# A two-layer graph convolution on one core: halved last chunk of each layer, and a prologue whose x reads, slot lists and order test stand elsewhere

## The reference

```python
norm = _cheb_norm(src, dst, x.shape[0])
h = jnp.maximum(_layernorm(x, axis=-1), 0.0)
# _cheb_conv(x, W0, W1, b): prop gathers h[src], scales by norm, sums by dst
out = x @ W0
tx1 = prop(x)
out = out + tx1 @ W1
return out + b
...
h = _cheb_conv(x, src, dst, norm, W1_0, W1_1, b1)
h = _layer_norm(h, gamma, beta)
h = jnp.where(h >= 0, h, NEG_SLOPE * h)
out = _cheb_conv(h, src, dst, norm, W2_0, W2_1, b2)
# the kernel returns x + out
```

## Time and profile before

| | us |
|---|---|
| median of three runs | 2506.06 |
| lowest, highest | 2500.96, 2516.93 |
| the profiled execution | 2524.07 |
| its span, first to last instruction | 2522.2 |

### The profile page before, as it was taken

The page is one execution under the profiler, slowest core; times in us unless marked ns, Lnnn a source line. Parts: engine busy times, 40 slices in busy tenths (PEclk is TensorE's granted clock), DMA queues, the critical chain, the costliest instruction groups (busy, mean ns, idle before and its releaser), DMA issues.

```text
span 2522.2 us, 25703 instructions
## 1 busy us (share of the span) xinstructions
PE 2030.6 (81%) x6734; PEld 1107.1 (44%) x6734; DVE 1412.3 (56%) x3392; ACT 1486.9 (59%) x2720; POOL 1491.0 (59%) x1574
## 2 busy tenths in 40 slices
PE   3358878888888788788877888787888888878787
PEld 3334434444444444444434444444444444444444
DVE  9736656666666666666654445354445454545444
ACT  8537656666666666666654555455555455555554
POOL 0166666666666666666636656666666666656662
PEclk9979999999999999899998889999999899989999
DMA  9977676766677677667747666666676667666662
GB/s 224 267 252 205 201 207 195 205 200 201 204 205 204 202 204 205 191 199 208 203 126 225 197 204 209 216 209 212 211 214 209 208 209 218 208 195 213 214 215 93
DMA packets 195754, 516.14 MB, mean 205 GB/s; under 512 B 44343, under 2 KB 46030, under 8 KB 195612
## 3 DMA queue, kind: packets, MB, share of 16 engines
q0 software_dynamic: 125120, 411.69, 55.7%
q1 hardware_dynamic: 67664, 102.43, 13.1%
q10 hardware_dynamic: 2828, 0.44, 0.1%
HBM read 473.61 MB, written 40.84 MB: 204 GB/s over the span
## 4 chain that ended last, share of the span: by engine, by line
ACT 28%; PE 24%; another core or an unknown queue 23%; issue 14%; DVE 7%; DMA 1%; SPq 1%; ACTq 0%; POOL 0%; DVEq 0%; POOLq 0%
PE ps L1161 12%; ACT high L629 7%; ACT ps L629 6%; ACT ps L630 5%; PE ps L1312 4%; ACT high L630 4%; PE ps L1305 3%; PE ps L1303 3%; DVE low L981 2%; ACT work L670 2%; DVE low L985 1%; ACT hots_full L581 1%; PE ps L1156 1%; PE ps L1248 1%
## 5 line engine op out<-in xcount | busy, mean ns | idle before, releaser
L525 POOL DMA_INDIRECT arena<-table,idx_all x1550 | 1473.7, 951 | 899.3 <-issue 486.1
L985 DVE TENSOR_TENSOR low<-arena,ps 128x512 fp32r<-128x512 f32 x517 | 339.0, 680 | 523.0 <-ACT ps L630 254.5
L1303 PE MATMUL ps<-high,hots 128*128 128x512 f32 x1034 | 583.1, 564 | 0.2 <-issue 0.2
L981 DVE SCALAR_TENSOR_TENSOR low<-arena,ps 128x512 fp32r<-128x512 f32 x517 | 372.5, 742 | 307.6 <-ACT ps L629 185.2
L1312 PE MATMUL ps<-arena,hots_full 128*128 128x512 f32 x1060 | 527.5, 596 | 0.0
L1305 PE MATMUL ps<-low,hots 128*128 128x512 f32 x1034 | 423.0, 409 | 50.5 <-DVE low L981 26.4
L629 ACT ACTIVATE high<-arena 128x512 fp32r<-128x512 f32 x517 | 368.0, 712 | 15.2 <-remote 15.2
L629 ACT ACTIVATE ps<-arena 128x512 fp32r<-128x512 f32 x517 | 354.2, 685 | 31.6 <-DMA arena<-table,idx_all 29.3
L630 ACT CAST ps<-arena 128x512 fp32r<-128x512 f32 x517 | 305.5, 591 | 87.6 <-DVE low L985 66.5
L1161 PE MATMUL ps<-arena 128*128 128x512 f32 x424 | 235.8, 708 | 133.5 <-ACT arena L662 128.1
L630 ACT CAST high<-arena 128x512 fp32r<-128x512 f32 x517 | 320.5, 620 | 0.0
(11 more groups left out here) (153 smaller groups left out, 1531.3 us busy)
## 6 DMA issues: line engine op xcount, KB each, us to landing
arena<-table SPq DMA_DIRECT2D x106, 256.0 KB
arena<-table,idx_all POOLq DMA_INDIRECT x1550
table<-arena SPq DMA_DIRECT2D x53, 256.0 KB
arena<-in_x_dram SPq DMA_DIRECT2D x53, 256.0 KB
out_dram<-arena SPq DMA_DIRECT2D x53, 256.0 KB
table<-arena SPq DMA_DIRECT2D x10, 1120.0 KB
arena<-in_x_dram SPq DMA_DIRECT2D x9, 1120.0 KB
w_all<-in_L_gnn_W_dram SPq DMA_DIRECT2D x2, 1024.0 KB
```

The costliest lines, as they stand in the source:

```text
L525: nc.gpsimd.indirect_dma_start(out=rows[u][:, c, 0:RW if L == 0 else D], out_offset=None, in_=table[L][0:NEAR if near else N, :], in_offse ...
L981: nc.vector.scalar_tensor_tensor(out=low[a], in0=rows[u][:, c, 0:D], scalar=rows[u][:, c, D:D + 1], in1=high_ps[s % NB][:, :], op0=ALU.mul ...
L985: nc.vector.tensor_tensor(low[a], rows[u][:, c, 0:D], high_ps[s % NB][:, :], ALU.subtract).then_inc(s_low, 1)
L1303: nc.tensor.matmul(tx_ps[u][:, :], hot, high[a], start=c == 0, stop=False)
```

## The change

The line numbers of the changed kernel differ. In the prologue, x groups 1 to 10 are read through GpSimd's queue; SyncE reads group 0 alone and has the slot lists between the table stores; `idx_all`, the order test and the bases stand ahead of the node scales on VectorE, and the transpose of `dst_rows` stands last on TensorE; GpSimd's wait for the table stands inside the branch.

```diff
@@ sync
-            for g in range(NG):
-                for n0, n1 in parts:
-                    sp.dma_start(nodes[n0:n1, XG[g]:XG[g + 1], :], x_rows[n0:n1, XG[g]:XG[g + 1], :],
-                                 max_dma_last_dim=4 * D).then_inc(s_x[g], 16)
+            for n0, n1 in parts:
+                sp.dma_start(nodes[n0:n1, XG[0]:XG[1], :], x_rows[n0:n1, XG[0]:XG[1], :],
+                             max_dma_last_dim=4 * D).then_inc(s_x[0], 16)
...
-            slot_rows(src, idx_all, s_idx)
-            slot_rows(dst, dst_rows, s_dsts)
             for g in range(1, NG):
+                if g == 3:
+                    slot_rows(src, idx_all, s_idx)
+                elif g == 5:
+                    slot_rows(dst, dst_rows, s_dsts)
@@ gpsimd
+            for g in range(1, NG):
+                for n0, n1 in ((0, TA), (TA, TR)):
+                    pool.dma_start(nodes[n0:n1, XG[g]:XG[g + 1], :], x_rows[n0:n1, XG[g]:XG[g + 1], :],
+                                   max_dma_last_dim=4 * D).then_inc(s_x[g], 16)
...
             bad = pool.value_load(flag_i[0:1, 0:1], min_val=0, max_val=1)
-            pool.wait_ge(s_tab, 2 * 16 * (NG - 1))
-            pool.wait_ge(s_factor_out, 48)
@@ gpsimd, layer(L) and general(L), L == 0
+                    pool.wait_ge(s_tab, 2 * 16 * (NG - 1))
+                    pool.wait_ge(s_factor_out, 48)
@@ vector
             nc.vector.reciprocal(factors[:, :, 0], sqrt_veps_deg).then_inc(s_factor, 1)
+            dve.wait_ge(s_idxps, 1)
+            nc.vector.tensor_copy(idx_all[:, 0:4 * P], src_ps[0][:, :]).then_inc(s_idxr, 1)
...
+            order()
+            bases()
```

```diff
+        def products(i, u):
+            if i < NC - 1:
+                return [(mm_ps[u][:, :], bass.ds(0, D))]
+            return [(mm_ps[u][:, 0:HD], bass.ds(0, HD)), (tx_ps[1 - u][:, 0:HD], bass.ds(HD, HD))]
@@ tensor
                     slots(i, u, h, 6, 11)
...
+                    if i == NC - 1:
+                        carried(L, u)
                     slots(i, u, h, 11, SLOTS)
...
-                    else:
-                        carried(L, u)
@@ scalar
                 chunks_of(act_step)
+                take_tx(L, NC - 1, 0)
+                copy_txT(L, NC - 1)
                 if L == 0:
                     make_sloped(NC - 2, 1)
-                take_tx(L, NC - 1, 0)
-                copy_txT(L, NC - 1)
@@ vector, finish2
-                nc.vector.scalar_tensor_tensor(out=mm_ps[u][:, :], in0=mm_ps[u][:, :], scalar=scale(i, 5),
-                                               in1=xin[u], op0=ALU.mult, op1=ALU.add).then_inc(s_res, 1)
...
-                nc.vector.tensor_tensor(stage, mm_ps[u][:, :], bias2, ALU.add).then_inc(s_fin, 1)
+            def residual2(i, u, h):
+                dve.wait_ge(s_xr[u], 16 * (h + 1))
+                nc.vector.tensor_tensor(xin[u], xin[u], bias2, ALU.add).then_inc(s_res, 1)
...
+                    last = nc.vector.scalar_tensor_tensor(out=stage[:, cols], in0=mm, scalar=scale(i, 5),
+                                                          in1=xin[u][:, cols], op0=ALU.mult, op1=ALU.add)
```

More of the change, by code:

```diff
@@ L524, in layer @@
                         n = first_slot(i) + c
+                        rn = REST if n == S - 1 else P
                         nc.gpsimd.indirect_dma_start(
-                            out=rows[u][:, c, 0:RW if L == 0 else D], out_offset=None, in_=table[L][0:NEAR if near else N, :],
+                            out=rows[u][0:rn, c, 0:RW if L == 0 else D], out_offset=None, in_=table[L][0:NEAR if near else N, :],
                             in_offset=bass.IndirectOffsetOnAxis(
-                                ap=(idx_near if near else idx_all)[:, n:n + 1].bitcast(U32), axis=0),
+                                ap=(idx_near if near else idx_all)[0:rn, n:n + 1].bitcast(U32), axis=0),
                         ).then_inc(s_gath[u][c], 16)
@@ L832, in tile_mean @@
                 dve.sem_inc(s_dpass, 1)
-                norm.add(nc.vector.bn_aggr(mv[0:TR, :], stats[0:TR, :]))
+                norm.add(nc.vector.bn_aggr(mv[0:TR, :], stats[0:TR, 0, :]))
             def tile_relu(t):
@@ L887, in _ @@
                                   dst_rows[0:S - FB * P, FB * P:]).then_inc(s_dstrows, 1)
-            order()
-            bases()
             dve.wait_ge(s_locps, 1)
@@ L1062, in norm1 @@
                 epi.settle(dve)
-                nc.vector.scalar_tensor_tensor(out=mm_ps[u][:, :], in0=mm_ps[u][:, :], scalar=veps[:, 1:2],
-                                               in1=bet, op0=ALU.mult, op1=ALU.add).then_inc(s_h1, 1)
-                assert epi.n == K_EPI
+                for mm, cols in products(i, u):
+                    nc.vector.scalar_tensor_tensor(out=mm, in0=mm, scalar=veps[:, 1:2], in1=bet[:, cols], op0=ALU.mult,
+                                                   op1=ALU.add).then_inc(s_h1, 1)
@@ L1067, in finish1 @@
+                assert epi.n == K_EPI + (3 if i == NC - 1 else 0)
             def finish1(i, u):
[L1069 to L1075 removed]
+                for n, (mm, cols) in enumerate(products(i, u)):
+                    dve.wait_ge(s_slope, i + 1 + n)
+                    if n == 0:
+                        dve.wait_ge(s_tab1, 16 * (i + 1))
+                    dve.sem_inc(s_dpass, 1)
+                    last = nc.vector.scalar_tensor_tensor(out=stage[:, cols], in0=mm, scalar=scale(i, 2),
+                                                          in1=sloped[:, cols], op0=ALU.mult, op1=ALU.max)
@@ L1088, in layer @@
+                last.then_inc(s_fin, 1)
             def layer(L):
@@ L1304, in slots @@
                             pe.wait_ge(s_low, split_no(L, i, c) + 1)
-                            last = nc.tensor.matmul(tx_ps[u][:, :], hot, low[a], start=False, stop=i == NC - 2 and c == SLOTS - 1)
+                            last = nc.tensor.matmul(tx_ps[u][:, :], hot, low[a], start=False, stop=i >= NC - 2 and c == SLOTS - 1)
                         else:
```

104 lines of the change are left out of this document (66 added, 38 removed).

## The result

| | before | after |
|---|---|---|
| median of 20 runs, us | 2515.24 | 2505.02 |
| lowest, highest | 2499.65, 2523.11 | 2482.57, 2518.61 |
| ratio, 95% interval | | 0.9963 (0.9947 to 0.9980) |
| span of the profiled execution | 2522.2 | 2480.7 |

The changed kernel is 0.37% faster, 9.3 us, and three further comparisons gave 0.9948 (0.9921 to 0.9976), 0.9969 (0.9947 to 0.9991) and 0.9960 (0.9936 to 0.9984): 0.40% on the mean of the four, 10 us. The forecast was −9.7 us, 0.39%. The spans differ by 41.5 us, but the trace of after is of the fastest of its 20 executions and that of before, 2524.07, is above all 20 of before, so they must be read place by place.

What follows compares the result with a forecast made beforehand. GpSimd's successive gathers were taken to fill the middle, with SyncE's late issues holding up the prologue. Terms of −6, −1.8 and −1.9 sum to −9.7 us, from a median of 2506.06 to 2496.4 us, range 2484 to 2510.

Steps and rivals of the forecast that it cites:

- no change: Whole kernel: a result within about 1%, 25 us, of before, given 0.84; faster by that 0.10, slower 0.06.
- The sum: Whole kernel: prologue −6, layer 0's end −1.8 and layer 1's end −1.9 make −9.7 us.
- Prologue, −6: Before the first gather: SyncE, freed of x reads, issues the factors at about 97, not 103.32; bounds −1 and −8.
- First slot: After the first gather: VectorE's later last step may hold the first slot back a microsecond, covered by gathers running on.
- The start is passed on: From prologue to total time: the prologue's −6 us enters the sum in full.
- Layer 0's end, −1.8: Layer 0's tail: earlier carry products −0.9, last operation in two halves −0.9; bounds −0.5 and −8.
- Layer 1's end, −1.9: Layer 1's tail: carry −0.9, one 256-column operation behind dense_tx −1.0; bounds −1 and −3.
- the DMA engines limit the prologue: Prologue: transfers, not SyncE's issues, set the end; only 1 to 3 us come through, about 2500; chance 0.25.
- GpSimd starved by VectorE: Prologue: x reads wait for one-hots, 9.2 us a group and no gain, or about 2540 at double price; chance 0.06.
- The residual add: Layer 1's chunks: the early add delays gather issues by up to 0.69 us each, about 2504, 2533 in full; chance 0.10.
- The fourth rival: Layer 0's end: the copy's remote wait and slow dense_tx both go, −3.2 and −3.1, about 2490; chance 0.20.

Runs made afterwards that it cites:

- pause_each: The changed kernel with one tiny GpSimd operation, waited for, after every gather; 1.0064 (1.0037 to 1.0090) of the kernel before.
- reads_only: The kernel before with only x groups 1 to 10 read through GpSimd's queue, SyncE reading group 0; 0.9975 (0.9958 to 0.9992) of before.
- prologue_only: The kernel before with only the change's edits ahead of the layers, the wait inside the branch among them; 0.9980 (0.9964 to 0.9997) of before.
- reads_back: The changed kernel with the x reads back on SyncE, ahead of the stores; 0.9961 (0.9946 to 0.9976) of before, then 0.9931 (0.9903 to 0.9958).
- near_late: The changed kernel with the 14 near gathers of layer 1's first chunk held until all of the table is stored; 1.0001 (0.9983 to 1.0018) of before.
- near_held: The changed kernel with the last six of 14 near gathers held until layer 0's last product; 0.9950 of before, and 0.9948 when run again (near_held_again).
- late_start: The changed kernel with 80 tiny GpSimd operations, each waited for, between the factors' landing and the first gather; 0.9987 (0.9969 to 1.0005) of before.
- after_again: The changed kernel itself run once more, nothing altered, as yardstick; 0.9948 (0.9921 to 0.9976) of the kernel before.

## Why the prediction was right or wrong

**The step that failed** is "about 1%, 25 us, is what a measurement of this kernel can tell from no change". By it the working's −9.7 us became "no change" with 0.84. The interval of 20 runs a side is ±0.17%, and the measured ratio, 0.9963 (0.9947 to 0.9980), lies clear of 1: the kernel is faster. The working itself had the bounds of all three terms below zero, −2.5 to −19 us; the statement to make was "faster, by 0.1 to 0.8%". In the sum, the term that was mis-sized is the prologue's.

**The sum** of −9.7 us came out: −10 over four comparisons. That it is so near is in part luck. Read from the traces, the parts are 4.3 us at the first gather (2.5 at the first slot, below), 2.3 and 2.0, together 7 to 9; and a mean of four comparisons is itself uncertain by some 3 us.

**Prologue, −6.** The chain was right: SyncE was the late one, its first store went out at 23.15 ("about 24"), its factors at 95.84 ("about 97"), the first gather at 110.24 ("near 111"). What failed is the size: "the factors go out at about 97 instead of 103.32" took one trace for the kernel. Over four traces the old prologue issues them at 98.75 to 103.32, and the gain at the first gather is 4.3 us on the mean. GpSimd's issue, estimated at 4.65 us a group from the gather, took 14.24 / 20 = 0.71 us a DMA: a gather's 7.4 ns a row doesn't carry over to a plain DMA. That error cost nothing, as it lay under cover.

**First slot.** By the working the first rows land at about 118 and VectorE's last step ends at about 119, and the microsecond between them was taken as covered by gathers that run ahead. ScalarE started on the gathered rows at 121.52 in this trace, 2.8 us earlier than before's 124.35, and at 118.9 to 121.4 in ten others; the means of the old and the new prologue are 122.6 and 120.1. So 2.5 of the 4.3 us are left at the first slot. VectorE's last step is what it stands behind: in all eleven traces of the new prologue without a pause, ScalarE starts 0.52 or 0.53 us after this row, where in the old one it waited for the rows.

```profile
121.00 0.29 DVE L977 COPY iota_i<-ps 128x128 f32<-128x128 f32 x1 [3.92 <-remote]
```

The row starts at 118.4 to 121.0 in the changed kernel's four traces and at 116.6 to 119.0 in before's three, some 2 us later, as forecast for the moved transpose. In the trace above a late release came on top, since TensorE had made the counts by 118.81; in the other three VectorE's wait there is 1.77 us, as in before.

**The start is passed on.** The sum took it in full. With a pause of 13.6 us, 7 to 10 came out, too uncertain to tell it from all of it; the time of `pause_each` says that gathers and slots both set the pace.

**Layer 0's end, −1.8.** The number was near, 2.3, by luck: the way to it was wrong. From VectorE's first pass to the start of the store's issue it was to be 4.4 us instead of 5.3; it is 5.44 (1306.39 to 1311.83), since the halves begin together there and each pass is issued twice. The gain lies ahead of it: from the last slot product to the end of the store's issue, carry included, it was 18.7, 19.2 and 18.6 us in the traces of before (the carry's 0.85 with 17.9, 18.3 and 17.8 behind it), and is 16.2 to 16.3. In two more kernels with the old ends, `reads_only` and `prologue_only`, it was 16.2 and 20.0, so the gain is 2.3 on the mean of five, and between nothing and 3.8 from trace to trace. The carry gives 0.85 of it, and the rest is the first pass waiting for the near gathers' end rather than for the whole of dense_tx.

**Layer 1's end, −1.9.** Right by its parts: the carry's 0.85, and from the copy of the transposes to the store's end 5.26 us (2473.34 to 2478.60) instead of 6.39 (2512.68 to 2519.07), 1.1 for one half pass in place of two whole ones.

**Rivals.** That the DMA engines limit the prologue fell as worked out: 307 GB/s went through where 226 had, and the 15 us ahead of the factors ran at a share of 0.55. The factors themselves took about as long as before: the first gather came 14.4 to 16.8 us after their issue in the changed kernel's four traces, 14.1 to 17.8 in before's three. Yet the rival's outcome, little gained from a second queue, holds for the reads by themselves (`reads_back`). The Trainium skill's page "Trainium Kernel Development and Optimization" (Key Constraints) says that issuing from several engines saves only the sequencer's issue time. The runs agree as far as they go: what was saved is SyncE's time, 46.60 us of it, for 14.24 of GpSimd's, and `reads_back`, which takes that back, is no slower. GpSimd starved by VectorE didn't occur: the first eight reads, ahead of VectorE's first one-hots at 7.67, took 0.74 us each, and the twelve beside them 0.70. The Trainium skill's page "SBUF — State Buffer" (Who interferes with whom) had inferred that operations with two on-chip inputs leave descriptor writing alone; these 0.70 us agree. The residual add held nothing up that the times show. The fourth rival named the two symptoms of layer 0's end, the remote wait and the slow dense_tx, and "nothing in the lists says why the wait should be gone" was so for this pair: it went from 3.93 to 2.75 with the gathers left where they were. With the gathers out of the tail it was gone in all three traces (`near_late`, `near_held`, `near_held_again`), and the tail shorter by up to 5.4 us. The slow dense_tx is a thing apart: it was there in one of the three.

## What to carry to other kernels

A start or an issue time read from one trace is a draw from a spread; where a term rests on it (here 103.32 in a spread of 98.75 to 103.32), look for a second trace or a second place that bounds it. Halving a last operation pays only where the release of the first half arrives on time: check in the trace how long releases of that engine take at that very place, and what runs on the others. Compare the forecast with the interval of the measurement it will meet, not with a round per cent.

## What the hardware showed

TensorE's releases can come late while indirect gathers run. In the same 14-slot kernel the copy behind four transposes starts 0.03 to 0.05 us after them with no gather about (layer 1's end, every trace), and up to 13.0 us after them with gathers being issued without a break. Not every release is late then: at layer 0's end of the changed kernel the copy came 2.03, 0.03, 0.66 and 0.66 us after the transposes, all with near gathers being issued, while the first pass was late in all four. With the gathers taken away from there, both releases were prompt in three traces of two kernels. That the gathers cause it is shown at that place; for the middle it is an inference. Whether it is their issue by GpSimd or the transfers of their rows isn't shown: the release came 2.44 to 2.63 us after the last issue ended, and which of the two ends then wasn't told apart. In `near_held` the copy was prompt with no gather being issued, though rows were still moving (DMA share 0.68 from the last slot's product to dense_tx), which speaks for the issue; but the prompt copies with gathers being issued keep it from being proof. Pauses of 0.1 us between gathers and one gate a chunk didn't help, so what a release needs to get through stays open, and with it some 540 us of remote waits on ScalarE in a kernel of 2500; how much of that is slack which something else would fill isn't known.

TensorE's clock is a matter of its own. The same dense_tx of two halves took 3.72 us at a granted clock of 1.00 and 5.41 at 0.69, with prompt and with late releases (`late_start` and `after_again`, both prompt, had one each), so two traces of the same rows can differ by 1.7 us for no reason in the code.
